# A four-stage transformer kernel: the second cross attention carries its queries and decode work over group borders, and the last layer becomes one stream

## The reference

```python
# cross attention, 16 heads of 128, 8 key/value heads
q = (text_hidden @ Wq)...; k = (vision_tokens @ Wk)...; v = (vision_tokens @ Wv)...
scores = jnp.where(mask, einsum('bhtd,bhsd->bhts', q, k) / scale, -inf)
attn = jax.nn.softmax(scores, axis=-1)
out = einsum('bhts,bhsd->bhtd', attn, v)... @ Wo
# feed-forward with weights that are looked up in a table of 16 values
w = lut[idx]                       # gate, up (688 x 256) and down (256 x 688)
h = jax.nn.silu(x @ gate.T) * (x @ up.T);  y = h @ down.T
x = x + tanh(g_xattn[1]) * attention(_layernorm(x), ctx);  x = x + tanh(g_ffn[1]) * ffn(_layernorm(x))
```

## Time and profile before

| | |
|---|---|
| median of 3 runs | 521.7 us |
| profiled execution, its own time | 521.62 us |
| its span (first to last instruction) | 519.8 us |
| mean granted clock of TensorE | 0.89 |
| PE busy | 436.0 us, 84% of the span |
| DVE / ACT / POOL busy | 352.4 / 199.7 / 173.2 us |
| stage C, first score matmul to last output | 282.39 to 454.39 us |
| stage D, first gate product to end of span | 456.05 to 519.8 us |

### The profile page before, as it was taken

How to read it: one execution, slowest core, us unless ns; L and a number is a source line. 1 busy time by engine, 2 the same in 40 slices (tenths; PEclk the granted TensorE clock), 3 DMA queues, 4 the chain that set the end, 5 groups by cost and what they waited for, 6 DMA issues and landing times.

```text
span 519.8 us, 9005 instructions
## 1 busy us (share of the span) xinstructions
PE 436.0 (84%) x3024; PEld 400.1 (77%) x3024; DVE 352.4 (68%) x769; ACT 199.7 (38%) x391; POOL 173.2 (33%) x207
## 2 busy tenths in 40 slices
PE   0465866958477999999998999989999998989996
PEld 0444856847367999999998988968987897788885
DVE  5767577584505668585855887798698879756642
ACT  2346445355220434343332443444354253423331
POOL 3104133231400221212134533653564355333332
PEclk9958785959657999999998969989987998999999
DMA  8111010100200020200101001001001000000000
GB/s 248 29 61 62 0 61 0 32 31 0 101 1 0 1 102 0 78 23 27 74 0 54 1 6 48 0 0 52 0 0 51 1 0 0 0 2 20 20 20 21
DMA packets 6629, 15.96 MB, mean 31 GB/s; under 512 B 1091, under 2 KB 4292, under 8 KB 6101
## 3 DMA queue, kind: packets, MB, share of 16 engines
q1 hardware_dynamic: 6612, 15.75, 9.2%
HBM read 14.70 MB, written 1.05 MB: 30 GB/s over the span
## 4 chain that ended last, share of the span: by engine, by line
PE 33%; issue 31%; POOL 15%; DVE 11%; ACT 6%; DMA 2%; POOLq 1%; DVEq 0%; ACTq 0%; SPq 0%
PE ps L289 19%; PE ps L484 5%; POOL workr L1010 4%; DVE work L1292 4%; PE ps L1086 3%; POOL work L1344 3%; POOL workr L1468 2%; PE ps L474 2%; POOL workA L565 2%; ACT workA L509 1%; POOL wB_lo L571 1%; POOL rstd L254 1%; PE ps L1098 1%; PE ps L359 1%; POOL wB_lo L1349 1%
## 5 line engine op out<-in xcount | busy, mean ns | idle before, releaser
L289 PE MATMUL ps<-xT_hi,wB_hi 128*128 128x256 f32 x224 | 65.7, 293 | 1.7 <-POOL wB_lo L1349 1.7
L289 PE MATMUL ps<-xT_lo,wB_hi 128*128 128x256 f32 x224 | 64.1, 286 | 0.0
L289 PE MATMUL ps<-xT_hi,wB_lo 128*128 128x256 f32 x224 | 63.9, 285 | 0.0
L289 PE MATMUL ps<-wB_hi,workr 128*128 128x256 f32 (+1 forms) x224 | 52.1, 296 | 4.5 <-POOL workr L1468 3.4
L289 PE MATMUL ps<-wN_hi,shared_r 128*128 128x256 f32 x256 | 52.8, 302 | 0.0
L1344 POOL TENSOR_SCALAR work<-work,lut_step,lut 128x344 f32<-128x344 int32 (+1 forms) x72 | 46.3, 659 | 1.7 <-POOL wB_lo L1349 1.6
L1010 POOL TENSOR_TENSOR workr<-work,workr 128x256 fp32r<-128x256 f32 (+1 forms) x36 | 22.9, 637 | 71.7 <-ACT workr L893 71.7
L1292 DVE COPY_PREDICATED work<-work 128x1376 f32<-128x1376 int32 (+5 forms) x36 | 43.6, 1212 | 4.0 <-DVE work L1292 1.1
L289 PEld LDWEIGHTS ps<-xT_hi,wB_hi 128*128 128x128 f32 x224 | 43.4, 194 | 2.4 <-issue 1.9
L289 PEld LDWEIGHTS ps<-wN_hi,shared_r 128*128 128x128 f32 x256 | 44.0, 206 | 1.5 <-DVE shared_r L1255 1.5
L289 PEld LDWEIGHTS ps<-wB_hi,workr 128*128 128x128 f32 (+1 forms) x224 | 38.4, 189 | 7.5 <-issue 6.2
(11 more groups left out here) (183 smaller groups left out, 1128.8 us busy)
## 6 DMA issues: line engine op xcount, KB each, us to landing
stage<-in_wC SPq DMA_DIRECT2D x4, 1280.0 KB, 5.5
stage<-in_wB SPq DMA_DIRECT2D x4, 768.0 KB, 4.3
stage<-in_idx SPq DMA_DIRECT2D x4, 536.0 KB, 4.0
stage<-in_wA SPq DMA_DIRECT2D x2, 512.0 KB, 5.4
out<-x SPq DMA_DIRECT2D x4, 256.0 KB, 2.2
x<-in_x SPq DMA_DIRECT2D x1, 768.0 KB, 6.7
ctx_T<-in_ctx_T SPq DMA_DIRECT2D x1, 512.0 KB, 7.1
ctx_n<-in_ctx_n SPq DMA_DIRECT2D x4, 128.0 KB, 2.1
```

What stands on the lines that cost most here:

```text
L289: last = nc.tensor.matmul(out, l, r, start=start and i == 0, stop=stop and i == 2)
```

## The change

In stage C the running maximum is no longer subtracted by DVE: DVE writes the negated maximum, and PE adds it to the scores in PSUM by a matmul with an identity (`shift`); ACT's exponential then reads PSUM. The mask matmul takes 128 rows (127 of them zero) instead of one. `mix` issues its matmuls in pairs, one on rows 0 to 63 and one on rows 64 to 127. The last four query pairs stand between the score parts; the first four of the next group stand before `output(1, ...)` of this one (`pe_C_query`), and in the last group the first three gate products of D stand there. The decode work is placed anew: POOL makes five candidates of each round and ACT three, `level1` is split, and it starts right after the bits are taken. D is written out four times, with the next group's first two gate products before this group's last two down products. The context of the next group and the indices are loaded and prepared a group ahead. The core of the diff:

```diff
-        def z_of(n):
-            return ps[:, (6, 7, 1)[n % 3], :]
+        def z_of(n, more):
+            return ps[:, (6, 7, 1, 5, 6, 0, 5, 4 if more else 7)[n], :]
...
+            def shift(u, s):
+                n = 2 * u + s
+                pe.wait_ge(*C["maxed"].at(g, n + 1))
+                nc.tensor.matmul(ps[:, 3 + s, :].rearrange("p (k n) -> p k n", k=8), ident_r, bc_last(neg_max[:, n, :], S),
+                                 start=False, stop=True, skip_group_check=True).then_inc(*C["shifted"].up())
...
-            queries(0)
-            scores(0)
-            queries(1)
-            turn_probs(0, 0)
-            turn_probs(0, 1)
-            scores(1)
-            mix(0)
-            turn_probs(1, 0)
-            output(0, 0)
-            turn_probs(1, 1)
-            output(0, 1)
-            front_pe(pe, 9 + g, 3)
-            mix(1)
-            output(1, 0)
-            output(1, 1)
+            scores(0, 0)
+            scores(0, 1)
+            shift(0, 0)
+            pe_C_query(pe, g, 4)
+            shift(0, 1)
+            pe_C_query(pe, g, 5)
+            pe_C_query(pe, g, 6)
+            pe_C_query(pe, g, 7)
+            turn_probs(0, 0)
+            turn_probs(0, 1)
+            scores(1, 0)
+            mix(0, 0)
+            mix(0, 1)
+            scores(1, 1)
+            shift(1, 0)
+            output(0, 0, first)
+            shift(1, 1)
+            output(0, 0, second)
+            output(0, 1, first)
+            turn_probs(1, 0)
+            turn_probs(1, 1)
+            front_pe(pe, 9 + g, 3)
+            output(0, 1, second)
+            mix(1, 0)
+            mix(1, 1)
+            x_split(pe, 9 + g)
+            if more:
+                for n in range(PAIRS1):
+                    pe_C_query(pe, g + 1, n)
+            else:
+                for k in range(3):
+                    pe_D_gate_up(pe, 0, k)
+            output(1, 0, every)
+            output(1, 1, every)
...
@@ act_C @@
+            exps(0, 0)
+            level1(0, (5, 6, 7))
             exps(0, 1)
...
+            act_C_query(act, g, 4)
+            act_C_query(act, g, 5)
+            act.wait_ge(*C["scores_done"].at(g, 2))
+            act_C_query(act, g, 6)
+            act_C_query(act, g, 7)
             upper_probs(0)
...
+                upper_z(1, 3)
+                upper_decoded(1)
+                act.wait_ge(*C["scores_done"].at(g, 3))
+                act_C_query(act, g + 1, 0)
+                level1(2, (5,))
+                act_C_query(act, g + 1, 1)
...
+                act_C_query(act, g + 1, 3)
+                act_C_context(act, g + 1)
+                upper_decoded(2)
...
@@ dve_C @@
             lower_probs(1)
+            front_lower(dve, 9 + g, 3)
+            choose(1, (0, 1, 2))
+            take_bits(2, (0,))
+            for k in range(BG):
+                lower_z(1, k)
             add(0)
+            take_bits(2, (1, 2, 3))
+            if more:
+                dve_C_context(dve, g + 1)
+            else:
+                dve_D_hidden(dve, 0, 0)
+                dve_D_hidden(dve, 0, 1)
+            choose(2, (0, 1, 2))
             add(1)
...
@@ pool_C @@
+            front_pool(pool, 9 + g)
+            level1(0, range(POOL_LEVEL1))
             scale(0)
+            level1(1, range(1, POOL_LEVEL1))
             lower(0)
-            level1(1)
+            level1(1, (0,))
             scale(1)
+            level1(2, range(1, POOL_LEVEL1))
             lower(1)
-            level1(2)
+            level1(2, (0,))
             lower(2)
...
         def pe_D(pe, g, more):
+            for k in range(2, FC):
+                if g or k > 2:
+                    pe_D_gate_up(pe, g, k)
+                else:
+                    pe.wait_ge(*C["dec_lo"].at(GROUPS, 0))
+                pe_D_down(pe, g, k - 2)
+                if more and k == FC - 2:
+                    front_pe(pe, 13 + g, 0)
+            if more:
+                x_split(pe, 13 + g)
+                pe_D_gate_up(pe, g + 1, 0)
+            pe_D_down(pe, g, FC - 2)
+            if more:
+                pe_D_gate_up(pe, g + 1, 1)
+            pe_D_down(pe, g, FC - 1)
```

486 lines of the change are left out of this document (260 added, 226 removed).

## The result

The changed kernel takes 506.3 us (median of 4 runs, 506.04 to 506.91), the kernel before 521.8 us on the same chip (521.37 to 522.42): a ratio of 0.970 (95% interval 0.968 to 0.972). The forecast was 501.0 us with a range of 495 to 512: the sign and the range hold, the number is 5.3 us too low. The profiled execution took 506.47 us, its span is 504.5 us.

A forecast was written before the change was run, and what follows sets the result against it. It took the decode chain through DVE, ACT and POOL, not the clock, to set C's turn. C from 282.7, three turns of 40.0 to 402.7, first down 444.8, D to 499.2, plus 1.8: 501.0 us, range 495 to 512.

The forecast's parts named there:

- 40.0 us a turn: Stage C: each of three group turns lasts 40.0 us, with bounds of 38.3 and 42.
- 0.8 and 1.2 a turn: Stage C: PE's two new waits for ACT's query copies in each turn, 0.8 and 1.2 us.
- forecast 38.3: Stage C: PE's own work in a turn after the change, 38.3 us, about as before.
- at 0.1 each at worst: Stage C: 128-row mask matmul costs nothing, at worst 0.1 us each, 0.4 a group.
- Mix in pairs ... saving 1.4: Stage C: paired mix matmuls share slots, 2.9 us instead of 4.3, saving 1.4; at worst nothing.
- The shift was costed at 0.3: Stage C: each of four shift matmuls on PE takes 0.3 us, 1.2 a group.
- Rival 2: Stage C: the clock goes on falling, as the transpose rule implies; costs 10 us, 511 us in all; chance 0.18.
- The border into D: Last C group into D: first down product about 42.1 us after the group's first score, after 2.2 us idle.
- three full groups of 13.5 (the border work is covered by the other group's product): Stage D: three groups of 13.5 us between down products, without the 1.5 us lost at each border.
- the prediction's own signs of being right: Turns of 39 to 41 us, short C waits, one 2 to 3 us wait before D's first down, D groups 13.5.
- Rivals 3 and 5: Stage C. 3: handovers, turns 42 to 42.5, 509 us, chance 0.18. 5: slower ring of engine lists, 525 us, chance 0.06.
- rival 3's sign of 90%: Stage C: DVE busy over 90% of a turn would show that handovers between in-order lists set the turn.

The follow-up runs named there:

- experiment 2: Changed kernel with the mask matmul cut back from 128 rows to one: 511.6 us, ratio 0.981.
- 3: Changed kernel with the mix matmuls in blocks of three, one batch after the other, instead of by turns: 505.7 us, ratio 0.970.
- 7: Changed kernel with the scores' shift by their maximum done on DVE again instead of by PE's matmul: 515.9 us, ratio 0.984.
- 5: Changed kernel with POOL's decode rounds in their old order, each round's candidates in one piece and scaling behind them: 509.4 us, ratio 0.972.
- experiment 11: Kernel before the change with only the mask matmul made 128 rows instead of one: 521.6 us, ratio 0.998.
- 12: Changed kernel with the carried query and gate products behind the output, and DVE's and ACT's lists fitted to that order: 540.8 us, ratio 1.033.
- experiment 1: Changed kernel with POOL's root for the next group's normalisation moved behind the first two lower halves of D: 496.4 us, ratio 0.951.
- experiment 10: Changed kernel with POOL's root moved back, last C group's DVE, ACT and POOL lists reordered, piece 3's gate product before D's first down product: 493.6 us, ratio 0.945.
- Experiments 4: Changed kernel with the carried query and gate products put back behind the output, other lists unchanged: 554.6 us, ratio 1.063.

## Why the prediction was right, and where it was off

**C was sized too long.** "40.0 us a turn" measured 38.18, 38.20 and 38.30, 114.7 us for three instead of 120.0. PE waits 0.4 us or less for a query copy, seven times in all, where the listing had 0.8 and 1.2 a turn. PE is busy for 37.4 to 37.5 of the forecast 38.3. The 128-row mask product, costed at nothing and "at 0.1 each at worst", saves instead: 0.2 to 0.3 a score part, 0.9 a group (experiment 2). "Mix in pairs ... saving 1.4" saves nothing (3). Twelve mix products take 1.6 from their first start to the next other product in either order, 3.2 a group: the 4.3 read for the kernel before was 1.1 too long, the 2.9 of the forecast 0.3 too short. The shift was costed at 0.3 and starts the next instruction after 0.2 to 0.3. What the shift buys is DVE's time, 5.2 us in C (7); the decode rounds 3.2 (5).

**Rival 2 fell.** The clock is 1.00 in all four groups of C, though both transpose blocks still stand ahead of score parts. The rule of the Trainium skill, page "TensorE: Matmul & The Clock Gate", section "Part 4: PE-mode transpose", weighed there with 10 us, does not show in this kernel's order. Its section "Part 1", which ties the falls to idle gaps, agrees with these runs in part. The clock fell behind every wait of 2.22 us or more at the first down product, and not behind the one of 0.82 there, nor behind 1.66 and 1.89 at the start of D in the kernel before and in experiment 11. Behind the waits of 2.39 and 2.38 us, which eight kernels have, it fell nine times of sixteen. Waits of about 1.5 us in C went either way (all four in experiment 11, none in 7 and 12). And of the falls in the kernel before with PE busy throughout, in two of its four groups, it says nothing; the other two groups' falls came behind waits of 1.39 and 0.99 us. Of all the traces from C's start on, these two alone show a fall without idle time of PE shortly before it. Why they are gone stays open: 128 rows alone put falls at waits in their place (11), and the one trace of the changed kernel with one row has none (2).

**The border into D held.** The first down product came 42.5 us after the last group's first score, 42.1 forecast; the wait ahead of it was 4.46 us instead of 2.2, with the outputs done 2 us earlier. Of it POOL's root in front is one part: without it 3.40. The chain choice, copy, lower half (the decoded one ends at 437.96 in experiment 1) is the rest, as forecast, but the lower half of D's piece 0 stands behind it on POOL, and that the prediction did not count; nor did it have a term for the half clock behind the wait.

**The step that failed** is "three full groups of 13.5 (the border work is covered by the other group's product)". PE's product does cover the border; POOL's list does not. The prediction counted PE's work in D and did not read where the root had gone in `pool_D`: from third place to the head, while DVE's statistics, which it waits for, stayed behind the last x addition. Two groups took 17.8 and 17.7, and with 13.49 for the third D took 49.0 us instead of 40.5. Experiment 1 moved that one line, and D from its first down product to the end went from 63.0 to 56.3 us: 6.7 of the 8.5. The other 1.8 is the half clock behind the first wait, put at nothing in the prediction; it was still there in experiment 1 (15.23 for the first group) and gone in experiment 10.

**The sum.** C's start +1.6 (284.34 against 282.7; across kernels with the same stages A and B it lies between 281.9 and 284.8, so this is not the change's), turns -5.3, last group +0.4, D +8.5, tail +0.1, launch and end +0.2: +5.5, which is 506.5 against 501.0. Two errors of opposite sign hid each other; that the forecast came within 5.3 us is partly luck. Three of the prediction's own signs of being right failed: turns of 39 to 41 us, one wait of 2 to 3 us ahead of the first down product, and D groups of 13.5.

**Rivals 3 and 5** did not come about. DVE was busy for 87 to 89% of a turn, just under rival 3's sign of 90%, and no turn was longer for it. No wait in C was over 0.4 us but the 1.3 for the x addition. Experiments 4 and 12 show how much hangs on the lists: with the same work in another order the time was 541 to 555 us.

## What to carry to other kernels

When an order is rewritten, read every engine's list for what stands at the head of each group: an instruction that waits for the group before holds all that is queued behind it, and a short one (0.69 us) cost 2.4 us of idle time in each of two groups here, with 1.9 us of half clock behind one of them. Work that only frees another engine (the shift on PE) pays on the engine that sets the lists, even where it costs on the busiest. And a product can be moved ahead of a wait into a hole: experiment 10 cut the hole from 2.22 to 0.82 us, the half clock behind it went, and 2.1 us were won.

## What the runs showed of the hardware that was not expected

- A matmul with 1 row and 512 bf16 columns took 0.31 us to the next start, one with 128 rows 0.23, and the sixteen products behind it 1.93 against 1.73 (both up to the next mask product).
- Matmuls of 64 rows on the two halves of the rows ran side by side whether by turns (twelve in 1.66 us) or in blocks of three (twelve in 1.67).
- Two waits of the same length, 2.39 and 2.38 us, at the same place of two groups with the same list: behind the first PE ran at the lower of its two clock levels, 1.2 GHz (0.50 from 460 to 462 us), behind the second at 2.4 GHz throughout. Of the eight kernels here with this pair of waits, seven show the half clock behind exactly one of the two (four behind the first, three behind the second), and experiment 7 behind both.
